# A four-stage per-sample pipeline on one Trainium2 core: the software-pipelined loop cut at another place, the gate's logits issued among the next scores, and two places where products and transposes are laid out differently

## The chip, the cores and the metric

The kernel runs on one core of a Trainium2 chip. The metric is the device time of one execution in microseconds (us); lower is better. The engines are named as the profile names them: PE (TensorE, matrix products), DVE (VectorE), ACT (ScalarE), POOL (GpSimd), and SP (SyncE, which here issues every DMA). Each engine works off its own queue strictly in order, and engines wait for one another on semaphores.

## The reference, cut to what matters

There are 16 samples of 256 tokens by 256 features. Each goes through four residual stages:

```
x = x + x @ W0[subject].T + b0[subject]                       # per-sample linear
x = x + zX*lap_x(x) + zY*lap_y(x) + zR*x*(1-x)                # Laplacian and reaction
q,k,v = projections;  w = softmax([q.k (masked), q.k_own]/4)  # 16 heads of width 16
x = x + (w @ v) @ Wo + bo
h_e = relu(x @ wi_e) @ wo_e, e = chosen, shared0, shared1     # three experts, 1024 wide
g = softmax(relu([h_e at token 0] @ g1) @ g2)                 # gate: three logits a sample
x = x + g0*h_chosen + g1*h_shared0 + g2*h_shared1
```

## The kernel before

Operands in float32 are split into a rounded "hi" part and a "lo" rest, and a product is three matmuls: hi*hi, lo*hi, hi*lo (L520 to L522). Splitting costs an ACT copy (hi) and a DVE or POOL subtraction (lo) for each tile.

Each engine has a list of stage names, written out by hand (`PE_BODY`, `ACT_BODY`, `DVE_BODY`, `POOL_BODY`, `SP_BODY`). One pass through the lists is a turn, and a turn works on up to three samples at once: `lag(name)` says how many samples behind the turn's number a stage is. Turns 0 and 1 are unrolled, turns 2 to 15 are a hardware loop (`Fori`), turns 16 and 17 are unrolled again. In the steady state every engine repeats its list once per sample.

The stages that matter:

- **S0 to S15**: the scores of one head, for the row maxima (PE L623, two matmuls; DVE L987 reduces them). After S7 and S15 DVE makes the maxima into three bf16 parts (L994 to L1000), **m0/m1** transposes them on PE, ACT copies them out, and SP's DMA L451 (`q_rows<-max_rows`) puts them under the queries. The first exponential of each half, E0 and E8, waits for that DMA (`max_placed`).
- **E0 to E15**: the scores again with mask and maxima (PE L636), then ACT's exponential twice (L833 in float32, L837 in float16; for heads 11, 13 and 15 DVE makes the float16 copy, L1006), and the rest `prob_lo` on DVE (heads 1, 3, 5, 7, 11, 13, 15; L1007) or POOL (the others; L1208). Right behind E(h) PE issues `attend(h-2)`, eight small matmuls that need `prob_lo` of head h-2.
- **H0 to H11 and P0 to P11**: the experts' first and second layer in twelve steps (12 products each). H(s) on ACT makes `hid_hi` (L873), on DVE `hid_lo` (L1067). H(s) on PE waits for the split of H(s-2), P(s) for that of H(s). Experts 0 and 1 are shared, steps 8 to 11 are the chosen one, whose weights are loaded for each sample.
- **wi0 to wi3, wo0 to wo3**: the chosen expert's weights. SP loads a quarter into `raw`, ACT makes `exp_hi` (L849), POOL `exp_lo` (L1151). The load of wo n (L403) goes into the place of wi n and waits until POOL has split it.
- **load**: SP's five DMAs for the next sample (weights, x, side input, bias, coefficients).
- **aT, wo, x3_parts**: attention's result is transposed on PE (L548), split with the bias (ACT L864, DVE L1048), multiplied with Wo, and added (DVE L1060); ACT L881 and DVE L1063 split that sum for the experts, and H0 waits for it.
- **gate, relu, logits, mix, scale, sum**: PE L696, DVE L1086, PE L701 (logits), DVE L1090 and L1091, ACT exponential, DVE L1095 to L1097 (mix), then DVE L1055 (scale), ACT L890 twice, POOL L1180 and L1182 (sum), and SP's store.
- **kp, k3** on SP: from the end of E15 SP issues 13 DMAs (mask, six `q_rows`, six `k_rows`) that place the next sample's queries and keys. S0 waits for all of them.

`RING` is the list of the PE stages that use the two banks `front0` and `front1` in turn (S, E, m, x1, q, lap, ks, vs, kp, vp, self). A stage waits until the stage two places before it in that list has been read out (`open_bank`).

The loop begins with H0 in every list. The order around the places that change is, before:

```
PE:  ... aT vp wo gate self logits | H0 S0 S1 H1 S2 S3 P0 S4 S5 H2 S6 S7 P1 H3 S8 S9 P2 m0 H4 S10 S11 P3 H5
     E0 S12 E1 P4 E2 S13 H6 E3 S14 P5 E4 S15 H7 E5 P6 E6 m1 ... E11 E12 kp E13 P9 E14 H11 E15 P10
SP:  ... k3 sum | load wo0 wo1 wo2 wo3 m0 m1 wi_load E15 kp k3 sum
POOL: ... ks vp sum | wi0 wi1 wi2 wi3 wo0 x_parts wo1 ...
```

Of the kernel before, what the change touches and what calls it, by code (L numbers as in the profile page):

```python
# [24 lines left out]
ACT = mybir.ActivationFunctionType  # L25
# [7 lines left out]
P = 128  # L33
# [21 lines left out]


PE_BODY = """
H0 S0 S1 H1 S2 S3 P0 S4 S5 H2 S6 S7 P1 H3 S8 S9 P2 m0 H4 S10 S11 P3 H5
E0 S12 E1 P4 E2 S13 H6 E3 S14 P5 E4 S15 H7 E5 P6 E6 m1 H8 E7
x1 P7 q E8 H9 E9 lap P8 E10 H10 E11 E12 kp E13 P9 E14 H11 E15 P10 ks pvend P11  # L60
vs aT vp wo gate self logits
""".split()
ACT_BODY = """
H0 wi0 x3_keep H1 wi1 H2 wi2 wi3 H3 wo0 m0 H4 wo1 x_parts P3 H5 w_parts E0 E1 wo2 E2 H6 E3 wo3 E4 H7 E5 s_parts E6 m1 H8 E7
x1_parts react q E8 P7 H9 E9 qa E10 x2_parts H10 E11 qb E12 kp E13 kq E14 H11 E15 ks P11
vs aT vp x3_parts x2b logits sum
""".split()
DVE_BODY = """
S0 S1 H0 S2 S3 H1 S4 S5 S6 H2 S7 S8 H3 S9 x_parts S10 H4 S11 S12 H5 E1 S13 gate0 H6 S14 E3 S15 H7 E5 H8 E7
x1 x1_parts react H9 half lap gate1 x2_parts H10 E11 kp E13 k3 H11 E15  # L70
att aT gate2 vp wo x3_parts relu self logits mix scale
""".split()
POOL_BODY = """
wi0 wi1 wi2 wi3 wo0 x_parts wo1 w_parts E0 wo2 E2 wo3 E4 s_parts E6 m1 x1 E8 E9 qa E10 norm qb E12 E14 ks vp sum
""".split()
SP_BODY = """
load wo0 wo1 wo2 wo3 m0 m1 wi_load E15 kp k3 sum
""".split()

S_OF, E_OF = [f"S{h}" for h in range(H)], [f"E{h}" for h in range(H)]  # L80
PRESENT = "load x_parts w_parts s_parts x1 x1_parts react q qa qb lap x2_parts ks vs kp kq k3 vp x2b self".split()
PREVIOUS = S_OF + E_OF + "m0 m1 half norm pvend att aT wo x3_parts wi_load".split()


def lag(name):
# [18 lines left out]

SHARED_AT = ["ks", "vp", "E0", "E2", "E4", "E6", "m1", "E8"]
SHARED = len(SHARED_AT)
SP_FIRST = "load wo0 wo1 wo2 wo3 m0 E0 E2 E4 E6 m1 wi_load E15 kp k3 vp sum".split()
assert [x for x in SP_FIRST if x in SP_BODY] == SP_BODY
LIN_ORDER = [0, 1, 2, 3]
PARTS = 2 * STEPS  # L110
# [17 lines left out]

BQ, BK, BO, BV, B_PREV, B_SELF, NVEC = range(7)

LINKS = {"early": 4, "attention": 4 + 5 + len(HI_DVE), "rest": 8}


def wait(eng, sem, per_turn, turn, n):
# [7 lines left out]
def build(nc, x, side, seq_len, subject, label, z, w0, b0, wqkvo, vecs, wi, wo, swi, swo,  # L142
          g1, g2, consts, iota, out):
    with ExitStack() as ctx:
# [233 lines left out]
        def _(sp):  # L378
# [43 lines left out]
            def stage(name, i):  # L422
# [10 lines left out]
                elif name == "E15":  # L433
                    wait_filled(sp, i, name)
                elif name == "kp":
                    sp.dma_start(k_rows[MASK_ROW:MASK_ROW + 1, :, :],
                                 mask_dram[bass.ds(i, 1), :].unsqueeze(1).to_broadcast([1, H, S])).then_inc(mask_placed, 16)
                    wait(sp, q_split, 1, i, 1)
                    place(q_rows, Q_BANDS, q_parts, 0, q_placed)
                    place(q_rows, Q_BANDS, q_parts, 1, q_placed)  # L440
                    place(q_rows, Q_BANDS, q_parts, 2, q_placed)
                    wait(sp, k_part_done, 2 * C, i, 2 * C)
                    place(k_rows, K_BANDS, k_parts, 0, k_placed)
                    place(k_rows, K_BANDS, k_parts, 1, k_placed)
                elif name == "k3":
                    wait(sp, k_split, 1, i, 1)
                    place(k_rows, K_BANDS, k_parts, 2, k_placed)
                elif name in ("m0", "m1"):
                    half = int(name[1])
                    wait_freed(sp, i, name)  # L450
                    sp.dma_start(q_rows[ROWS_MAX:ROWS_EXP, half * HALF:(half + 1) * HALF, :], max_rows[:, :]).then_inc(max_placed, 16)  # L451
                elif name == "wi_load":
                    kind = chooser(label_sb, i, wi.shape[0])
                    wait(sp, w_split, PARTS, i, SHARED)
                    load_wi(kind)
                elif name[0:2] == "wo":
# [60 lines left out]
        def _(pe):  # L517
# [124 lines left out]
            def hidden(s, j):  # L642
# [110 lines left out]
        def _(act):  # L753
# [158 lines left out]

        @block.vector
        def _(dve):
            link_sems = {"early": early_link, "attention": attention_link, "rest": rest_link}
            linked = dict.fromkeys(LINKS, 0)

            def link(ins, stretch, seq):
# [121 lines left out]
            def rest(name, j):  # L1040
# [238 lines left out]
```

## Time and profile before

| | |
|---|---|
| median of three runs | 1175.02 us (1174.24 to 1176.38) |
| the profiled execution | 1179.7 us, of which the span of its instructions 1177.9 us |
| PE busy (matmuls) | 1028.2 us, 87% of the span |
| PE weight loads | 955.5 us, 81% |
| DVE | 818.1 us, 69% |
| ACT | 682.4 us, 58% |
| POOL | 634.3 us, 54% |

Busy shares are averages over the whole span. Matmuls are pipelined, so PE's busy time is not time at its peak. The clock column of a view is the granted TensorE clock, 1.00 for 2.4 GHz and 0.50 for 1.2 GHz. A releaser behind "<-" is what ended an engine's idle time.

### The profile page before, as it was taken

The numbers are of one execution on the slowest core, as the hardware profiler recorded it, in microseconds if no ns is written. First come the engines' busy times: TensorE is split into PE (matmuls) and PEld (weight loads), VectorE is DVE, ScalarE is ACT, GpSimd is POOL, SyncE is SP. The second block draws the span as 40 slices with busy tenths as digits, with TensorE's granted clock in tenths as the row PEclk, the third lists the DMA queues.
The fourth block names the chain that finished last, engine by engine and source line by source line (L and its number), as shares of the span: only waits on it lengthen the run. The fifth ranks groups of instructions, "written<-read, shape, count | busy, mean of one in ns | idle before, by whom it ended". The sixth has DMA issues, their size and how long they took to land.

```text
span 1177.9 us, 27595 instructions
## 1 busy us (share of the span) xinstructions
PE 1028.2 (87%) x9488; PEld 955.5 (81%) x9488; DVE 818.1 (69%) x1616; ACT 682.4 (58%) x1401; POOL 634.3 (54%) x544
## 2 busy tenths in 40 slices
PE   3658989999898999899899999989989998998986
PEld 3347878888888888888788888878888887888886
DVE  3475776777777777767777776777777777867632
ACT  2463655747466564746566574656657475665632
POOL 5492645637464564736466473646647364654531
PEclk8667998999999999999999999999999999999978
DMA  4636152171524216152522615242251624234110
GB/s 137 114 108 99 45 67 72 37 124 36 63 77 70 78 47 115 36 69 82 64 72 52 109 36 83 78 54 72 58 104 36 91 70 54 72 63 73 38 45 9
DMA packets 91387, 82.67 MB, mean 70 GB/s; under 512 B 11972, under 2 KB 90852, under 8 KB 91364
## 3 DMA queue, kind: packets, MB, share of 16 engines
q1 hardware_dynamic: 91364, 82.37, 34.8%
q8 instruction: 14, 0.23, 0.1%
q14 instruction: 9, 0.07, 0.0%
HBM read 52.58 MB, written 4.20 MB: 48 GB/s over the span
## 4 chain that ended last, share of the span: by engine, by line
POOL 30%; issue 27%; PE 23%; DVE 13%; ACT 5%; DMA 1%; POOLq 1%; SPq 0%; DVEq 0%; ACTq 0%
POOL exp_lo L1151 10%; POOL prob_lo L1208 10%; PE out L520 3%; DVE prob_lo L1007 3%; PE out L522 3%; PE out L521 3%; PE hid L520 2%; PE hid L521 2%; PE hid L522 2%; PE front L520 2%; POOL e_out L1180 2%; PE front L522 2%; PE front L521 1%; POOL s_lo L1161 1%; PE pv L578 1%
## 5 line engine op out<-in xcount | busy, mean ns | idle before, releaser
L520 PE MATMUL hid<-x_hi,exp_hi 128*128 128x256 f32 x768 | 239.9, 312 | 1.4 <-DVE x_lo L1063 1.4
L1208 POOL TENSOR_TENSOR prob_lo<-prob,prob_hi 128x512 f16<-128x512 f32 x144 | 182.8, 1270 | 88.3 <-ACT prob_hi L837 87.1
L520 PE MATMUL out<-hid_hi,exp_hi 128*128 128x256 f32 x768 | 229.2, 298 | 0.0
L522 PE MATMUL hid<-x_hi,exp_lo 128*128 128x256 f32 x768 | 225.7, 294 | 0.0
L521 PE MATMUL hid<-x_lo,exp_hi 128*128 128x256 f32 x768 | 225.7, 294 | 0.0
L1151 POOL TENSOR_TENSOR exp_lo<-raw,exp_hi 128x512 fp32r<-128x512 f32 x128 | 163.8, 1290 | 109.7 <-ACT exp_hi L849 109.7
L987 DVE TENSOR_REDUCE s_max<-front 128x2 f32<-128x512 f32 x256 | 171.6, 687 | 68.9 <-PE front L623 67.1
L521 PE MATMUL out<-hid_lo,exp_hi 128*128 128x256 f32 x768 | 215.4, 280 | 0.0
L522 PE MATMUL out<-hid_hi,exp_lo 128*128 128x256 f32 x768 | 215.2, 280 | 0.0
L873 ACT ACTIVATE hid_hi<-hid 128x512 fp32r<-128x512 f32 x192 | 115.4, 601 | 168.4 <-PE hid L522 167.0
L1067 DVE SCALAR_TENSOR_TENSOR hid_lo<-hid,hid_hi 128x512 fp32r<-128x512 f32 x192 | 131.5, 685 | 104.0 <-ACT hid_hi L873 102.2
L833 ACT ACTIVATE prob<-front 128x512 f32<-128x512 f32 x256 | 153.2, 599 | 33.6 <-PE front L636 32.4
L520 PEld LDWEIGHTS hid<-x_hi,exp_hi 128*128 128x128 f32 x768 | 154.7, 201 | 5.6 <-DVE x_lo L1063 1.5
L521 PEld LDWEIGHTS hid<-x_lo,exp_hi 128*128 128x128 f32 x768 | 155.5, 202 | 0.0
L522 PEld LDWEIGHTS hid<-x_hi,exp_lo 128*128 128x128 f32 x768 | 154.3, 201 | 0.0
L520 PEld LDWEIGHTS out<-hid_hi,exp_hi 128*128 128x128 f32 x768 | 145.4, 189 | 3.8 <-DVE hid_lo L1067 1.9
L521 PEld LDWEIGHTS out<-hid_lo,exp_hi 128*128 128x128 f32 x768 | 145.6, 190 | 0.0
L522 PEld LDWEIGHTS out<-hid_hi,exp_lo 128*128 128x128 f32 x768 | 145.2, 189 | 0.0
L1007 DVE TENSOR_TENSOR prob_lo<-prob,prob_hi 128x512 f16<-128x512 f32 x112 | 112.9, 1008 | 36.7 <-ACT prob_hi L837 35.1
L636 PE MATMUL front<-q_rows,k_rows 100*128 100x256 bf16 x512 | 102.7, 284 | 32.7 <-ACT prob_hi L837 29.2
L837 ACT ACTIVATE prob_hi<-front 128x512 f16<-128x512 f32 x208 | 125.1, 602 | 0.0
L578 PE MATMUL pv<-v_cols,prob_hi 128*128 128x49 bf16 x1024 | 86.8, 186 | 21.2 <-DVE prob_lo L1007 10.6
(162 smaller groups left out, 2311.1 us busy)
## 6 DMA issues: line engine op xcount, KB each, us to landing
raw<-in_wi SPq DMA_DIRECT2D x64, 256.0 KB, 3.7
raw<-in_wo SPq DMA_DIRECT2D x64, 256.0 KB, 2.9
q_rows<-w_raw SPq DMA_DIRECT2D x80, 128.0 KB, 4.3
k_rows<-x1T SPq DMA_DIRECT2D x48, 128.0 KB, 6.6
k_rows<-x_raw SPq DMA_DIRECT2D x48, 128.0 KB, 7.9
x_raw<-in_x SPq DMA_DIRECT2D x16, 256.0 KB, 3.1
w_raw<-in_w SPq DMA_DIRECT2D x16, 256.0 KB, 2.8
s_raw<-in_side SPq DMA_DIRECT2D x16, 256.0 KB, 3.7
```

Of the source, the lines that this page charges most:

```text
L520: nc.tensor.matmul(acc, w_hi, a_hi, start=first, stop=False)
L521: nc.tensor.matmul(acc, w_hi, a_lo, start=False, stop=False)
L522: return nc.tensor.matmul(acc, w_lo, a_hi, start=False, stop=last)
L636: last = nc.tensor.matmul(psum[:, k * S:(k + 1) * S], k_rows[0:ROWS_EXP, h, k * P:(k + 1) * P], q_rows[0:ROWS_EXP, h, :], start=True, stop ...
L833: last = nc.scalar.activation(prob[:, h % NPROB, :], psum[:, :], ACT.Exp, scale=SCALE)
L837: last = nc.scalar.activation(prob_hi[:, h % NPROB, :], psum[:, :], ACT.Exp, scale=SCALE)
L873: nc.scalar.activation(hid_hi[:, s % 2, :], hid_bank[s % 2][:, :], ACT.Relu).then_inc(hid_hi_done, 1)
L987: nc.vector.tensor_reduce(s_max[:, :, h:h + 1], psum, AX_X, ALU.max).then_inc(freed["S"], 1)
L1007: nc.vector.tensor_tensor(prob_lo[:, h % NPROB, :], prob[:, h % NPROB, :], prob_hi[:, h % NPROB, :], ALU.subtract).then_inc(prob_split_dve, 1)
L1067: nc.vector.scalar_tensor_tensor(hid_lo[:, s % 2, :], hid_bank[s % 2][:, :], 0.0, hid_hi[:, s % 2, :].bitcast(F32), ALU.max, ALU.subtract) ...
L1151: nc.gpsimd.tensor_tensor(lo, source, hi.bitcast(F32), ALU.subtract).then_inc(w_split, 1)
L1208: nc.gpsimd.tensor_tensor(prob_lo[:, h % NPROB, :], prob[:, h % NPROB, :], prob_hi[:, h % NPROB, :], ALU.subtract).then_inc(prob_split_poo ...
```

## The change

Three things are done at once.

**The loop is cut elsewhere.** H0 to H3, P0, P1 and S0 to S7 with all that belongs to them move from the start of each list to its end, with their lags lowered by one, so the steady order of most stages is the same and the turn's boundary lies between H3 and S8. Around it some orders do change: on PE the logits go from before H0 to behind S1; on DVE logits, mix and scale are spread among S0 to S4; on POOL sum goes from ahead of wi0 to between wi1 and wi2; on ACT it goes behind H1; and SP issues the four loads of wo ahead of the store, and only then `load` for the next sample and m0's DMA.

**Exponentials are spaced by products.** P4 goes between E0 and E1, and H6, P5, H7 and P6 between the following ones, which leaves E5, E6 and m1 next to each other. Later P9 goes between E11 and E12, and H11 between E13 and E14, which leaves E14 and E15 next to each other. DVE's x_parts goes behind H7, its gate1 behind x2_parts. ACT's w_parts goes behind E1.

**Attention is turned over two banks.** The four transposes write both halves of `pv` in place of one bank, ACT signals after each half, and DVE starts on the first half while ACT copies the second.

```diff
 PE_BODY = """
-H0 S0 S1 H1 S2 S3 P0 S4 S5 H2 S6 S7 P1 H3 S8 S9 P2 m0 H4 S10 S11 P3 H5
-E0 S12 E1 P4 E2 S13 H6 E3 S14 P5 E4 S15 H7 E5 P6 E6 m1 H8 E7
-x1 P7 q E8 H9 E9 lap P8 E10 H10 E11 E12 kp E13 P9 E14 H11 E15 P10 ks pvend P11
-vs aT vp wo gate self logits
+S8 S9 P2 m0 H4 S10 S11 P3 H5 E0 S12 P4 E1 S13 H6 E2 S14 P5 E3 S15 H7 E4 P6 E5 E6 m1 H8 E7
+x1 P7 q E8 H9 E9 lap P8 E10 H10 E11 P9 E12 kp E13 H11 E14 E15 P10 ks pvend P11
+vs aT vp wo gate self H0 S0 S1 logits H1 S2 S3 P0 S4 S5 H2 S6 S7 P1 H3
 """.split()
 ACT_BODY = """
-H0 wi0 x3_keep H1 wi1 H2 wi2 wi3 H3 wo0 m0 H4 wo1 x_parts P3 H5 w_parts E0 E1 wo2 E2 H6 E3 wo3 E4 H7 E5 s_parts E6 m1 H8 E7
-x1_parts react q E8 P7 H9 E9 qa E10 x2_parts H10 E11 qb E12 kp E13 kq E14 H11 E15 ks P11
-vs aT vp x3_parts x2b logits sum
+m0 wo0 H4 wo1 x_parts P3 H5 E0 E1 w_parts H6 E2 wo2 E3 H7 wo3 E4 E5 s_parts E6 m1 H8 E7
+x1_parts react q E8 P7 H9 E9 qa E10 x2_parts H10 E11 qb E12 kp E13 kq H11 E14 E15 ks P11
+vs aT vp x3_parts x2b H0 logits wi0 H1 sum wi1 x3_keep H2 wi2 wi3 H3
 """.split()
 DVE_BODY = """
-S0 S1 H0 S2 S3 H1 S4 S5 S6 H2 S7 S8 H3 S9 x_parts S10 H4 S11 S12 H5 E1 S13 gate0 H6 S14 E3 S15 H7 E5 H8 E7
-x1 x1_parts react H9 half lap gate1 x2_parts H10 E11 kp E13 k3 H11 E15
-att aT gate2 vp wo x3_parts relu self logits mix scale
+S8 S9 S10 H4 S11 S12 H5 E1 S13 gate0 H6 S14 E3 S15 H7 x_parts E5 H8 E7
+x1 x1_parts react H9 half lap x2_parts gate1 H10 E11 kp E13 k3 H11 E15
+att aT gate2 vp wo x3_parts relu self S0 S1 logits H0 S2 mix S3 H1 scale S4 S5 S6 H2 S7 H3
 """.split()
 POOL_BODY = """
-wi0 wi1 wi2 wi3 wo0 x_parts wo1 w_parts E0 wo2 E2 wo3 E4 s_parts E6 m1 x1 E8 E9 qa E10 norm qb E12 E14 ks vp sum
+wo0 x_parts wo1 E0 w_parts E2 wo2 E4 wo3 s_parts E6 m1 x1 E8 E9 qa E10 norm qb E12 E14 ks vp wi0 wi1 sum wi2 wi3
 """.split()
 SP_BODY = """
-load wo0 wo1 wo2 wo3 m0 m1 wi_load E15 kp k3 sum
+load m0 m1 wi_load E15 kp k3 wo_load0 wo_load1 wo_load2 wo_load3 sum
 """.split()
...
+PRESENT += S_OF[:HALF]
-PREVIOUS = S_OF + E_OF + "m0 m1 half norm pvend att aT wo x3_parts wi_load".split()
+PREVIOUS = S_OF[HALF:] + E_OF + """m0 m1 half norm pvend att aT wo x3_parts x3_keep H0 H1 H2 H3 P0 P1
+wi_load wi0 wi1 wi2 wi3 wo_load0 wo_load1 wo_load2 wo_load3""".split()
...
-                transposed(pv_bank[0], att).then_inc(att_turned, 1)
+                transposed(pv, att).then_inc(att_turned, 1)
...
-                    psum = chunked(pv_bank[0])
-                    for c in range(C):
-                        last = nc.scalar.activation(ak_hi[:, c, :], psum[:, c, :], ACT.Identity, bias=vec[:, c, BV:BV + 1])
-                    last.then_inc(att_hi_done, 1)
+                    for c in range(C):
+                        nc.scalar.activation(ak_hi[:, c, :], pv[:, c, 0:S], ACT.Identity, bias=vec[:, c, BV:BV + 1]).then_inc(att_hi_done, 1)
...
-                    wait(dve, att_hi_done, 1, j, 1)
-                    psum = chunked(pv_bank[0])
-                    for c in range(C):
+                    for c in range(C):
+                        wait(dve, att_hi_done, C, j, c + 1)
```

Waits for the shared experts' weights are put at the first step of each, in place of one wait at H0; after the first sample they are long met.

## Rows read from the trace of the kernel before

**Rows 1.** Busy time of each engine in one steady turn (windows)

```profile
437.00:505.20 68.20, 62.28 (x593) 58.41 (x593) 50.47 (x100) 41.98 (x88) 37.97 (x33) 0.97 0.36 70
```

**Rows 2.** Timeline of PE: E15 of two samples, one turn apart

```profile
437.54 0.39 PE L636 MATMUL front<-q_rows,k_rows 100*128 100x256 bf16 x2
...
505.80 0.39 PE L636 MATMUL front<-q_rows,k_rows 100*128 100x256 bf16 x2
```

**Rows 3.** Timeline of PE: logits, H0, S0, m0, E0

```profile
451.50 0.82 PE L701 MATMUL out<-gate,gate_h 128*128 128x3 f32 x4 [1.69 <-DVE gate_h L1086]
452.19 0.56 PE L520 MATMUL hid<-x_hi,exp_hi 128*128 128x256 f32 x1
...
454.90 0.74 PE L623 MATMUL front<-k_rows,q_rows 97*128 97x256 bf16 x4
...
466.10 0.28 PE L629 MATMUL front<-ident_half,m_parts 128*24 128x128 bf16 x2
...
471.13 0.39 PE L636 MATMUL front<-q_rows,k_rows 100*128 100x256 bf16 x2
```

**Rows 4.** Windows: H0, with the granted clock third from the end

```profile
451.70:455.10 3.40, 3.40 (x17) 3.27 (x17) 1.68 (x6) 1.54 (x3) 0.00 (x0) 0.51 0.26 24
```

**Rows 5.** SP's last `k_rows` issues, and landing of the tile's DMAs

```profile
444.72 1.90 SPq L420 DMA_DIRECT2D k_rows<-x_raw  x3
...
DMA to landing us min/median/max: 2.1/7.0/8.1
```

**Rows 6.** Timeline of SP: store, `load`, the wo loads, m0's DMA

```profile
457.93 0.42 SPq L463 DMA_DIRECT2D out<-e_out  x1
...
459.87 0.39 SPq L390 DMA_DIRECT2D w_raw<-in_w  x1
...
463.31 3.97 SPq L403 DMA_DIRECT2D raw<-in_wo  x4
467.42 0.86 SPq L451 DMA_DIRECT2D q_rows<-max_rows  x1
```

**Rows 7.** The chain that ended last: m0's DMA, issue to landing

```profile
50.98 2.31 DMA q_rows<-max_rows
```

**Rows 8.** Timeline of POOL: sum, then wi0 and wi1

```profile
455.12 1.28 POOL L1180 TENSOR_TENSOR e_out<-e_out 128x512 f32<-128x512 f32 x1 [4.68 <-ACT e_out L890]
...
457.72 2.52 POOL L1151 TENSOR_TENSOR exp_lo<-raw,exp_hi 128x512 fp32r<-128x512 f32 x2
```

**Rows 9.** Timeline of DVE around the logits and the first scores

```profile
450.36 0.69 DVE L1063 TENSOR_TENSOR x_lo<-x3T,x_hi 128x512 fp32r<-128x512 f32 x1 [0.70 <-ACT x_hi L881]
...
453.05 0.16 DVE L1095 TENSOR_REDUCE gate_s<-gate_s 128x1 f32<-128x3 f32 x1 [0.27 <-ACT gate_s L878]
...
453.71 0.75 DVE L1055 SCALAR_TENSOR_TENSOR e_out<-e_out,gate_s,x_kept 128x512 f32<-128x512 f32 x1
455.46 1.29 DVE L987 TENSOR_REDUCE s_max<-front 128x2 f32<-128x512 f32 x2 [1.00 <-PE front L623]
```

**Rows 10.** Timeline of PE: E1, kp, E13, attend(11)

```profile
473.47 0.39 PE L636 MATMUL front<-q_rows,k_rows 100*128 100x256 bf16 x2 [1.73 <-ACT prob_hi L837]
...
499.71 0.36 PE L520 MATMUL front<-x_hi,lin_hi 128*128 128x256 f32 x1 [1.14 <-DVE x_lo L929]
...
501.22 0.40 PE L636 MATMUL front<-q_rows,k_rows 100*128 100x256 bf16 x2
...
502.13 0.20 PE L578 MATMUL pv<-v_cols,prob_hi 128*128 128x49 bf16 x1 [0.51 <-DVE prob_lo L1007]
```

**Rows 11.** Timeline of DVE: gate0, E3, gate1, x2_parts

```profile
477.06 1.27 DVE L1082 SCALAR_TENSOR_TENSOR gate_terms<-gate,e_out,gate_terms 128x256 f32<-128x256 f32 x1
...
479.65 1.78 DVE L1007 TENSOR_TENSOR prob_lo<-prob,prob_hi 128x512 f16<-128x512 f32 x1
...
496.02 2.40 DVE L1082 SCALAR_TENSOR_TENSOR gate_terms<-gate,e_out,gate_terms 128x256 f32<-128x256 f32 x2
498.46 1.10 DVE L929 TENSOR_TENSOR x_lo<-react,x_hi 128x512 fp32r<-128x512 f32 x1
```

More of the change, by code:

```diff
@@ L106 @@
 SHARED = len(SHARED_AT)
-SP_FIRST = "load wo0 wo1 wo2 wo3 m0 E0 E2 E4 E6 m1 wi_load E15 kp k3 vp sum".split()
+SP_FIRST = "load m0 E0 E2 E4 E6 m1 wi_load E15 kp k3 vp wo_load0 wo_load1 wo_load2 wo_load3 sum".split()
 assert [x for x in SP_FIRST if x in SP_BODY] == SP_BODY
@@ L129 @@
 BQ, BK, BO, BV, B_PREV, B_SELF, NVEC = range(7)
-LINKS = {"early": 4, "attention": 4 + 5 + len(HI_DVE), "rest": 8}
+LINKS = {"early": 4, "maxima0": 2, "maxima1": 2, "attention": 5 + len(HI_DVE), "rest": 8}
 def wait(eng, sem, per_turn, turn, n):
@@ L328, in build @@
         early_link = sem("early_link")
+        maxima_link = [sem("maxima0_link"), sem("maxima1_link")]
         attention_link = sem("attention_link")
@@ L455, in stage @@
                     load_wi(kind)
-                elif name[0:2] == "wo":
-                    n = int(name[2])
+                elif name[:-1] == "wo_load":
+                    n = int(name[-1])
                     kind = chooser(label_sb, i, wo.shape[0])
@@ L547, in transposed @@
                     for t in range(C):
-                        last = nc.tensor.transpose(psum[:, c * S + t * P:c * S + (t + 1) * P],
-                                                   src[:, t, c * P:(c + 1) * P], ident[:, :])
+                        last = nc.tensor.transpose(psum[:, c, t * P:(t + 1) * P], src[:, t, c * P:(c + 1) * P], ident[:, :])
                 return last
@@ L647, in hidden @@
                     wait(pe, x3_split, 1, j, 1)
-                    pe.wait_ge(w_split, SHARED)
                     pe.wait_ge(gate_in, 32)
+                if s % STEPS == 0 and e < CHOSEN:
+                    pe.wait_ge(w_split, 4 * e + 2)
                 if e == CHOSEN:
@@ L666, in project @@
                 wait(pe, hid_split, LSTEPS, j, s + 1)
+                if s % STEPS == 0 and e < CHOSEN:
+                    pe.wait_ge(w_split, 4 * e + 4)
                 if s == 0:
@@ L914, in _ @@
         def _(dve):
-            link_sems = {"early": early_link, "attention": attention_link, "rest": rest_link}
+            link_sems = {"early": early_link, "maxima0": maxima_link[0], "maxima1": maxima_link[1], "attention": attention_link, "rest": rest_link}
             linked = dict.fromkeys(LINKS, 0)
@@ L925, in linkf @@
                 def linkf(ins):
-                    link(ins, "early" if name in EARLY else "attention", i)
+                    link(ins, "early" if name in EARLY else f"maxima{int(name[1:]) // HALF}" if name[0] == "S" else "attention", i)
                 def rest_of(src, hi, lo):
@@ L1044, in rest @@
                 if name == "aT":
-                    wait(dve, att_hi_done, 1, j, 1)
-                    psum = chunked(pv_bank[0])
                     for c in range(C):
-                        last = nc.vector.scalar_tensor_tensor(ak_lo[:, c, :], psum[:, c, :], vec[:, c, BV:BV + 1],
+                        wait(dve, att_hi_done, C, j, c + 1)
+                        last = nc.vector.scalar_tensor_tensor(ak_lo[:, c, :], pv[:, c, 0:S], vec[:, c, BV:BV + 1],
                                                               ak_hi[:, c, :].bitcast(F32), ALU.add, ALU.subtract)
```

## The prediction

> **What bounds the kernel now.** I read the page first, then one steady turn in windows, then the timelines of PE, DVE, ACT, POOL and SP through that turn, and SP's landings. The reader is to see three things. First, PE is the engine that sets the turn: busy 62.28 of 68.20 us, DVE 50.47, ACT 41.98, POOL 37.97 [rows 1]. The turn is 505.80 - 437.54 = 68.26 us [rows 2], and 13 of the 16 samples go through it in full. Second, PE's few waits are where the change aims. The logits wait 1.69 us for the gate, and H0 behind them starts at 452.19 [rows 3], in a stretch of 3.40 us granted 0.51 of the clock, the lower level of 1.2 GHz [rows 4]. E1 waits 1.73 us for ACT, kp 1.14 for DVE, attend(11) 0.51 for DVE [rows 10]. Third, two things that no wait of PE shows, since they are just hidden: SP's DMAs for queries and keys, and SP's place in line for m0's DMA.
>
> **Part 1, from E15 to S0: gains 0.7 us a turn, not 3.** Before, S0 stands 454.90 - 437.54 = 17.36 us after E15 [rows 2, 3]. With the logits behind S1, H0 waits only for the split of its input, which DVE ends at 450.36 + 0.69 = 451.05 [rows 9]; H0 takes 1.5 us at the full clock (twelve products, as kp's 499.71 to 501.22 [rows 10]). So S0 could come at 452.6, 2.3 us earlier, and turning attention over two banks would bring a few tenths on top. But S0 also waits for the DMAs. The last of the `k_rows` issues starts at 444.72 + 1.90 - 0.60 = 446.0 and lands 8.1 us later [rows 5], at 454.1, that is 16.6 us after E15; that series begins when E15 is filled, in the new order too. So S0 comes at E15 + 16.65: -0.7 us. The earlier H0, the two banks (they lie ahead of this landing, so I cost them at nothing; without that cover they gain up to 0.4) and H0's half clock (1.3 us, hidden too) all end at this one DMA. Bounds: 0 to -0.8.
>
> **Part 2, from S0 to E0: loses 4.0 us.** Before it is 471.13 - 454.90 = 16.2 us [rows 3]. Follow the new order, times after S0. DVE reduces S0 and S1 from 0.56 to 1.85 [rows 9]; the logits' two small steps end near 2.3 and H0's rest near 2.9. PE has issued logits (0.5) and H1 (1.5), so S2 reaches DVE at 2.95 and is reduced at 3.6; mix takes 453.71 - 453.05 = 0.66 [rows 9], so the gate stands at 4.25. Behind that:
>
> - POOL does wi1 only after ACT, whose list has sum's two scalings first. They took 455.12 - 453.71 = 1.4 us from the gate to POOL [rows 8, 9], so 5.65; ACT's wi1 0.6, to 6.25. POOL: wi1 1.26, sum 457.72 - 455.12 = 2.6, wi2 and wi3 2.52 [rows 8]: 6.25 + 1.26 + 2.6 + 2.52 = 12.65.
> - SP may issue the last wo load only then. Behind it in SP's queue stand the store, `load` with five DMAs, and m0's DMA. From the store's issue to the first wo load it now takes 463.31 - 457.93 = 5.4 us, with the look-up of 0.9 that belongs to wo; then the four wo loads, 467.42 - 463.31 = 4.1 [rows 6]. New: one wo load's issue 0.6, and 5.4 - 0.9 + 0.1 = 4.6 to m0's. So m0's DMA goes at 12.65 + 5.2 = 17.85, wherever the maxima are.
> - It lands 2.31 later [rows 7], at 20.15. E0 waits for it: E0 at 20.2, against 16.2: +4.0.
>
> PE alone would be slower here too: logits 0.5, and S5, S6 and S7 wait some 0.35 each for banks, because DVE has mix and scale (0.75 [rows 9]) between the reductions; that makes m0 stand near 12.6 instead of 466.10 - 454.90 = 11.2 [rows 3], and E0 could go at 17.6. That is the lower bound, +1.4; the upper one is +4.6 (SP at 5.8). I take +4.0, since POOL's and SP's work is counted piece by piece from rows. Behind the waiting E0 in PE's queue stand S12, P4 and everything else. The same delay of `load` holds up ACT's x_parts, and P3 and H5 behind it, until near 19.5; that is just hidden by E0's wait.
>
> **Part 3, from E0 to x1: between -1.9 and +1.0, taken +0.4.** E1's wait of 1.73 [rows 10] goes, since P4 fills it: about -1.9 with its start. But taking P4 ahead of E1 leaves less PE work behind E1 for DVE to catch up. From E1 DVE does prob_lo, S13, gate0, H6 and S14, which ended at 479.65 [rows 11], 6.2 us after E1 at 473.47 [rows 10]. S15 needs that bank, and PE now comes to it 4.4 us after E1; DVE is then some 0.5 faster, since S13 waits less, so about 1.35 is given back. Then E4, E5, E6 and m1 come with P6 alone between them: ACT has H7 and wo3's copy (0.6 each) ahead of E4, then POOL 1.2 for its rest, and attend(4) behind E6 waits about 1.0.
>
> DVE's times here swing: prob_lo was 1.78 us at 479.65 while POOL worked, and gate0's step 1.27 [rows 11]. The Trainium skill says in "SBUF — State Buffer", section "Who interferes with whom", that a DVE instruction with two SBUF inputs contends with a GpSimd instruction that reads SBUF; the trace's long ones agree. By that rule moving DVE's and POOL's work onto each other costs up to 1.1 a time, and part 3 would be +1.0.
>
> **Part 4, from x1 to E15: -0.75 us.** Up to E10 nothing moves. Before, kp waits 1.14 for `x_lo`, which stood behind gate1 (2.40 us from 496.02), and attend(11) waits 0.51 [rows 10, 11]. New: P9 goes ahead of E12 and x2_parts ahead of gate1, so kp waits for nothing. But attend(11) needs DVE's E11, and DVE's list up to there is the same work with an idle start, up to 0.9 until ACT's copy is there: attend(11) comes at best as now, at worst 0.9 later. Behind it one product fewer (1.5) stands before E15. So -1.5 to -0.5; I take -0.75. H11, E14 and E15 then follow with nothing waiting.
>
> **Sum.** -0.7 + 4.0 + 0.4 - 0.75 = +2.95 us a turn, to 71.2. Sample 2 to 14 see it in full: 13 x 2.95 = 38. Of the others, S0's sample 1 has no sum yet and sample 15 no `load` (about +1 each), and the last sample's tail, with no scores, gains 1.5 from the earlier H0. Together +39. The profiled execution, 1179.7 us (span 1177.9 and 1.8 around it), would become 1218.7. It lies 4.7 above the median of the three runs, so against 1175.0 I get 1214 us. The waits at S0 (2 us) and E0 (2.5 us) are new idle time of PE, and products behind such a wait can run at the lower clock, as H0 does today [rows 3, 4]; one such stretch costs 1.3 when nothing hides it. I add 2 us for a tenth of them and forecast 1216.
>
> **The rivals, and the forecast among them.**
>
> - **The forecast (0.50):** 1200 to 1230, by the bounds of the parts.
> - **The clock makes it worse (0.13).** Idle before the logits preceded the 3.40 us at 0.51 [rows 3, 4]. Two waits of that length a turn, each followed by dense products, cost 1.3 each: up to 13 x 2.6 = +34, and with one 13 x 1.3 = +17: 1231 to 1248. For it: E0's wait is longer than today's 1.69. Against: E1's wait of 1.73 today is followed by no low clock (the turn as a whole is at 0.97 [rows 1], which the one stretch explains). The Trainium skill, "TensorE: Matmul & The Clock Gate", section "HAM oscillation — how this bites in real kernels", describes a loop whose waits for DMAs throttle the products behind each of them; by it this rival is what would happen.
> - **Spacing pays in full (0.20).** Parts 3 and 4 at their best, -1.9 and -1.5: -0.7 + 4.0 - 1.9 - 1.5 = -0.1 a turn; with one of the two at its best, about +0.8 to +2: 1176 to 1200. For it: E1's wait is plain to see. Against: DVE's catching up.
> - **Faster (0.13).** SP's queue is not what E0 waits for: m0's DMA goes by 15.3 after S0 (17.6 - 2.31), so 2.5 us sooner than I count, for example because sum on POOL ends before wi1 is there. Then part 2 is +1.4 and the turn -0.7 + 1.4 + 0.4 - 0.75 = +0.35, and it turns to a gain from the point where part 3 gives back less than 1.5 of its 1.9; at best -0.7 + 1.4 - 1.9 - 1.5 = -2.7 a turn, 1140. Against: SP's order is fixed, and its issues have a measured length.
> - **No change within 0.2% (0.04)**, which is about what a measurement of this kernel can tell: gains and losses cancel.
>
> **Range and chances.** The cases from 1180 up to 1243 hold 8 in 10: it leaves out the faster rival and the far end of the clock's. Slower by over 0.2%: 0.50 + 0.13 + nearly all of 0.20 = 0.82; same 0.05; faster 0.13.
>
> **What would show it.** S0 waits for the DMA `k_rows<-x_raw`, with H0 ended well before. E0 waits 2 to 3 us for `q_rows<-max_rows`, whose issue follows `load`'s DMAs on SP without a pause. The logits don't wait. E1 doesn't wait, S15 and attend(4) wait for DVE and POOL. kp doesn't wait, attend(11) does. The turn is near 71 us. I am wrong if E0 doesn't wait, or if S0 comes less than 16.5 us after E15.

## The result and the profile after

The changed kernel takes 1277.5 us (median of four, 1258.5 to 1278.9) against 1175.7 for the kernel before. The ratio is 1.077, 95% interval 1.062 to 1.092; it leaves out two of the four runs, 1278.7 and 1278.9, which count as slow beside the 1258.5. Slower was right, the size was not: 1216 was forecast, with 1243 as the upper end. The profiled execution has a span of 1274.4 us against 1177.9, 96.5 more.

Where it went is read from PE's timeline, by the starts of the same instructions in each turn. The table has medians over 12 steady turns; "warm" is e7_warm (below), the changed kernel with PE kept busy in two waits. The forecast's E0 is taken as m0 + 7.6 (20.2 - 12.6).

| stretch, us | before | forecast | after | warm |
|---|---|---|---|---|
| E15 to aT | 6.8 | | 7.3 | 6.8 |
| aT to S0 | 10.5 | | 9.8 | 10.0 |
| (E15 to S0) | 17.3 | 16.65 | 17.1 | 16.8 |
| S0 to m0 | 11.2 | 12.6 | 16.1 | 14.3 |
| m0 to E0 | 5.0 | 7.6 | 6.5 | 6.5 |
| E0 to x1 | 15.0 | 15.4 | 15.2 | 15.2 |
| x1 to E15 | 19.7 | 18.9 | 20.3 | 19.3 |
| turn | 68.2 | 71.2 | 75.1 | 72.2 |

PE's timeline of one turn after; it answers to [rows 3, 10]:

```profile
478.93 0.38 PE L522 MATMUL hid<-x_hi,exp_hi 128*128 128x256 f32 x1 [1.28 <-DVE x_lo L1064]
...
482.36 1.03 PE L624 MATMUL front<-k_rows,q_rows 97*128 97x256 bf16 x4 [1.36 <-DMA k_rows<-x_raw]
483.19 0.85 PE L705 MATMUL out<-gate,gate_h 128*128 128x3 f32 x4
...
498.48 0.28 PE L630 MATMUL front<-ident_half,m_parts 128*24 128x128 bf16 x2 [1.91 <-DVE s_max L989]
...
505.04 0.39 PE L637 MATMUL front<-q_rows,k_rows 100*128 100x256 bf16 x2 [1.36 <-DMA q_rows<-max_rows]
...
517.76 0.20 PE L579 MATMUL pv<-v_cols,prob_hi 128*128 128x49 bf16 x1 [0.83 <-POOL prob_lo L1209]
...
537.36 0.20 PE L579 MATMUL pv<-v_cols,prob_hi 128*128 128x49 bf16 x1 [1.81 <-DVE prob_lo L1009]
```

The waits named in the prediction are there: S0 for the keys' DMA, E0 for the maxima's, S15 for DVE (0.4, and S14 as much), attend(4) for POOL, attend(11) for DVE; logits, E1 and kp don't wait. E0's is 1.36 us and not the 2 to 3 that were named, because another wait stands ahead of it that was not expected at this size: m0, 1.91 us for DVE.

The same turn in windows, the granted clock third from the end; it answers to [rows 1, 4]:

```profile
472.60:547.80 75.20, 65.31 (x593) 60.24 (x592) 51.08 (x100) 41.99 (x87) 37.61 (x33) 0.93 0.32 63
478.90:480.00 1.10, 1.07 (x9) 1.07 (x10) 0.47 (x3) 0.05 (x1) 0.00 (x0) 1.00 1.15 116
480.10:486.80 6.70, 5.34 (x26) 4.75 (x25) 2.18 (x5) 1.32 (x3) 1.28 (x1) 0.50 0.07 6
486.90:538.00 51.10, 43.91 (x427) 40.27 (x426) 37.24 (x67) 32.74 (x66) 32.57 (x28) 1.00 0.21 62
538.10:541.40 3.30, 3.30 (x29) 2.96 (x28) 2.33 (x5) 1.99 (x5) 0.00 (x0) 0.50 0.00 0
```

Before, 3.4 us of a turn ran at 1.2 GHz. Now it is 6.7 us around S0, and 3.3 us more behind the wait of attend(11). The first stretch begins at 480.1, inside H0, 1.2 us behind H0's wait and ahead of S0's; it holds all of S0's wait and reaches through H1 behind it.

SP's timeline, as [rows 6]: from the last wo load to m0's DMA it waits for nothing, 502.41 - 497.04 = 5.4 us. ACT had the maxima ready at 499.25 (second fence), 3.2 us ahead of that DMA.

```profile
497.04 0.38 SPq L405 DMA_DIRECT2D raw<-in_wo  x1
497.62 0.40 SPq L465 DMA_DIRECT2D out<-e_out  x1
499.76 0.39 SPq L392 DMA_DIRECT2D w_raw<-in_w  x1
...
501.93 0.34 SPq L396 DMA_DIRECT2D z_sb<-in_z  x1
502.41 0.87 SPq L453 DMA_DIRECT2D q_rows<-max_rows  x1
```

```profile
498.88 0.37 ACT L828 ACTIVATE max_rows<-front 24x256 bf16<-24x256 bf16 x1 [3.52 <-PE front L630]
```

DVE and POOL while DVE takes the first half's maxima apart (timelines of each):

```profile
493.25 1.03 DVE L996 SCALAR_TENSOR_TENSOR s_max<-s_max,s_self 128x16 f32<-128x16 f32 x1
494.32 1.21 DVE L998 TENSOR_SCALAR m_parts<-s_max 128x16 bf16<-128x16 f32 x1
495.56 1.21 DVE L999 SCALAR_TENSOR_TENSOR m_rest<-s_max,m_parts 128x16 f32<-128x16 f32 x1
496.69 0.16 DVE L1000 SCALAR_TENSOR_TENSOR m_parts<-s_max,m_parts 128x16 bf16<-128x16 f32 x1
```

```profile
491.58 1.30 POOL L1181 TENSOR_TENSOR e_out<-e_out 128x512 f32<-128x512 f32 x1
492.95 1.30 POOL L1183 TENSOR_TENSOR e_out<-e_out 128x512 f32<-128x512 f32 x1
494.21 2.53 POOL L1152 TENSOR_TENSOR exp_lo<-raw,exp_hi 128x512 fp32r<-128x512 f32 x2
```

Steps of 16 elements a partition take 1.0 to 1.2 us while POOL works, and end when POOL's instruction ends (494.28 and 494.25; 496.77 and 496.74). With POOL free the next one takes 0.16.

### The profile page after: what moved, and what is told of

Read it like the earlier page. It is cut to its first block, busy times and chain, and to the rows that moved or that the text cites. A ratio compares the mean times of both kernels' runs of the same rounds, so it can differ in the third digit from the quotient of the medians.

```text
span 1274.4 us, 27693 instructions
## 1 busy us (share of the span) xinstructions
PE 1068.2 (84%) x9488; PEld 982.6 (77%) x9488; DVE 826.0 (65%) x1616; ACT 681.8 (53%) x1401; POOL 627.4 (49%) x544
## 4 chain that ended last, share of the span: by engine, by line
issue 35%; PE 29%; POOL 19%; DVE 8%; ACT 4%; DMA 2%; SPq 1%; POOLq 1%; ACTq 0%; DVEq 0%
POOL exp_lo L1152 9%; PE hid L522 4%; POOL prob_lo L1209 3%; PE hid L524 3%; PE hid L523 3%; PE front L637 2%; PE out L522 2%; DVE prob_lo L1009 2%; PE out L523 2%; PE out L524 2%; PE front L522 2%; PE front L524 2%; PE front L523 2%; DMA k_rows<-x_raw 2%; PE pv L579 2%
## 5 line engine op out<-in xcount | busy, mean ns | idle before, releaser
L522 PE MATMUL hid<-x_hi,exp_hi 128*128 128x256 f32 x768 | 245.4, 319 | 21.1 <-DVE x_lo L1064 21.1
L1209 POOL TENSOR_TENSOR prob_lo<-prob,prob_hi 128x512 f16<-128x512 f32 x144 | 173.5, 1205 | 179.1 <-ACT prob_hi L841 178.4
L524 PE MATMUL hid<-x_hi,exp_lo 128*128 128x256 f32 x768 | 233.7, 304 | 0.0
L523 PE MATMUL hid<-x_lo,exp_hi 128*128 128x256 f32 x768 | 232.0, 302 | 0.0
L522 PEld LDWEIGHTS hid<-x_hi,exp_hi 128*128 128x128 f32 x768 | 159.5, 208 | 26.6 <-DVE x_lo L1064 22.7
L524 PEld LDWEIGHTS hid<-x_hi,exp_lo 128*128 128x128 f32 x768 | 161.2, 210 | 0.0
L523 PEld LDWEIGHTS hid<-x_lo,exp_hi 128*128 128x128 f32 x768 | 160.9, 210 | 0.0
L624 PE MATMUL front<-k_rows,q_rows 97*128 97x256 bf16 x512 | 101.9, 310 | 43.1 <-DMA k_rows<-x_raw 25.2
L579 PE MATMUL pv<-v_cols,prob_hi 128*128 128x49 bf16 x1024 | 90.5, 190 | 51.3 <-DVE prob_lo L1009 31.7
L579 PEld LDWEIGHTS pv<-v_cols,prob_hi 128*128 128x128 f16 x1024 | 75.3, 100 | 69.1 <-DVE prob_lo L1009 36.4
```

What stands on the lines that cost most here:

```text
L522: nc.tensor.matmul(acc, w_hi, a_hi, start=first, stop=False)
L523: nc.tensor.matmul(acc, w_hi, a_lo, start=False, stop=False)
L524: return nc.tensor.matmul(acc, w_lo, a_hi, start=False, stop=last)
L579: nc.tensor.matmul(acc, prob_hi[:, h % NPROB, at:at + P], v_cols[:, k, h, :], start=(k == 0), stop=False)
L624: last = nc.tensor.matmul(psum[:, t * S:(t + 1) * S], q_rows[0:ROWS_MAX, h, t * P:(t + 1) * P], k_rows[0:ROWS_MAX, h, :], start=True, stop ...
L1209: nc.gpsimd.tensor_tensor(prob_lo[:, h % NPROB, :], prob[:, h % NPROB, :], prob_hi[:, h % NPROB, :], ALU.subtract).then_inc(prob_split_poo ...
```

## The experiments

Ratios are to the kernel before, run beside each on the same chip. Stretches are medians over 12 steady turns, as in the table.

### One part of the change at a time

All four have the loop cut between H3 and S8.

**e1_cut**: the cut alone.

```diff
-PE:  ... gate self H0 S0 S1 logits H1 ...        (as changed)
+PE:  ... gate self logits H0 S0 S1 H1 ...        (all orders as before)
-SP:  load m0 ... k3 wo_load0..3 sum
+SP:  load wo_load0..3 m0 ... k3 sum              (wo_load two samples behind)
```

> Only the loop is cut between H3 and S8; all orders of work around it are those of before (save that DVE does H3 ahead of S8), attention turned in one bank. If the loss comes from the orders, the cut is free: 1175 us, within 6. Rival, the new cut costs something itself, because every engine now branches in the middle of dense work: 0.5 us or more for each of 14 turns, 1182 us or more.

Measured 1193.2 us, ratio 1.013 (1.009 to 1.017). The rival's size, but see e5_cut_s8 and e9b_cut_warm.

**e2_spacing**: e1_cut with the changed orders from S8 to P11.

> The cut kernel with the exponentials spaced by products (PE, ACT, DVE and POOL orders between S8 and P11 as in the change), logits and SP as before. Prediction's parts 3 and 4: -0.35 us a turn, 1170 us. Rival, DVE's late E11 brings a wait of attend(11) of 1.8 us and products at 1.2 GHz behind it, as the changed kernel's trace shows: +1.0 us a turn, 1188 us.

Measured 1204.2, 1.024 (1.021 to 1.028), 11 us above e1_cut. Neither number, the rival's mechanism: in turns without slow products behind attend(11), x1 to E15 takes 19.3 us, 0.4 less than before; in the others 20.4.

**e3_logits**: e1_cut with the changed orders from self to H3 on every engine, SP's too.

> The cut kernel with the logits among the next scores, sum between wi1 and wi2 on POOL and the wo loads ahead of the store and load on SP, as in the change; exponentials and attention as before. If nearly all of the loss is here (late m0 DMA and two stretches at 1.2 GHz around S0): +5.9 us a turn, 1250 us. Rival, the loss is shared with the spacing: by the prediction's parts 1 and 2, +3.3 a turn, 1218 us.

Measured 1293.5, 1.100 (1.096 to 1.104), above both numbers: all of the loss is here, and more than all. S0 to m0 takes 15.7 us, m0 to E0 8.0. At least a part of the excess over the changed kernel is not the logits' doing. DVE here still has x_parts between S9 and S10, as before, and waits there for the late `load`; E0 then waits for DVE and not for the maxima (one turn):

```profile
508.23 0.15 DVE L938 TENSOR_SCALAR z_neg<-z_sb 128x1 f32<-128x1 f32 x1 [4.95 <-DMA z_sb<-in_z]
...
510.76 0.39 PE L637 MATMUL front<-q_rows,k_rows 100*128 100x256 bf16 x2 [1.20 <-DVE s_max L991]
```

The changed kernel has x_parts behind H7, and DVE doesn't wait for `load` ahead of E0.

**e4_banks**: e1_cut with attention turned over two banks.

> The cut kernel with attention turned over two banks and nothing else. With the logits ahead of H0 the split of attention lies on PE's path: 0.4 us a turn, 1169 us. Rival, hidden: 1175 us.

Measured 1199.2, 1.018 (1.015 to 1.021), no better than e1_cut, so neither number, since the cut had cost something already. H0 does come 0.36 us sooner after aT (7.23 in place of 7.59), but S0 stands at 10.0, where the keys land.

**e5_cut_s8**: e1_cut, and DVE does S8 ahead of H3 again.

```diff
-DVE: ... S6 H2 S7 H3 | S8 S9 ...
+DVE: ... S6 H2 S7 | S8 H3 S9 ...
```

> The cut alone as in e1_cut, but DVE does S8 ahead of H3 again, as before the change. In e1_cut the stretch from S0 to m0 grew from 11.2 to 12.1 us and nothing else in the median turn. If that is DVE's H3 ahead of S8 (m0 needs the bank that S8 frees): 11.2 again and 1176 us. Rival, the branch of the loop between H3 and S8 costs it: 12.1 stays and so does 1190 us.

Measured 1202.2, 1.023 (1.020 to 1.025): the expectation failed, and so did the rival. In its short turns S0 to m0 is 11.5, so the order on DVE was a part; but more turns are long (seven of twelve, four in e1_cut). A short turn and the long one behind it, in windows, and the long one's stretch right behind E1's wait:

```profile
307.10:375.70 68.60, 62.39 (x594) 58.35 (x593) 50.23 (x100) 42.14 (x87) 38.16 (x33) 0.98 0.36 69
375.70:447.30 71.60, 65.40 (x593) 61.28 (x592) 49.72 (x100) 42.02 (x87) 38.21 (x33) 0.93 0.34 66
...
406.80:410.10 3.30, 3.30 (x18) 3.08 (x18) 0.69 (x1) 1.60 (x3) 2.40 (x3) 0.50 0.00 0
```

The same instructions, DVE, ACT and POOL equally busy within 0.6 us, and 3.0 us apart, which is PE's extra busy time. The long turns have slow products behind S0 (S0 to m0 12.7) and behind E0 (E0 to x1 16.5 in place of 15.0). E1's wait is 1.7 us in all twelve turns, and the clock falls behind it in seven. This asks for a test of the clock by itself.

### The clock by itself

The added products write the idle second hidden bank (at E1 the first) from constant weights.

```diff
+def keep_busy(n):
+    for _ in range(n):
+        nc.tensor.matmul(hid_bank[1][:, 0:S], lin_hi[:, 0, 0:P], lin_hi[:, 0, 0:S], start=True, stop=True)
...
+keep_busy(8)     # at S0, ahead of the wait for its DMAs
+keep_busy(12)    # at attend(11), ahead of its wait
```

**e7_warm**: the changed kernel with these two.

> The changed kernel with added products that nothing reads, in two of PE's waits: 8 ahead of S0's wait for its DMAs and 12 ahead of attend(11). If the low clock behind those two waits costs time of its own: S0 to m0 1.3 us and E14 to aT 1.4 us shorter, 13 x 2.7 = 35 us less: 1241 us. Rival, the slow products only fill time that DVE, POOL and SP would make PE wait anyway: 1270 us or more.

Measured 1238.2, 1.053 (1.051 to 1.056), the expectation. 20 useless products a turn make the kernel 39 us faster than its median and its profiled execution (span 1235.6 for 1274.4), and 20 faster than its one run at 1258.5. That run is itself a sign of the clock: its mean granted clock was 0.924, that of the other three 0.900 to 0.909. The turn is 72.2, its clock 0.98 in place of 0.93:

```profile
461.00:533.40 72.40, 65.20 (x614) 60.92 (x612) 51.20 (x100) 41.77 (x87) 37.62 (x33) 0.98 0.34 66
```

SP's last wo load, m0's DMA and E0 in that turn, whose S0 starts at 471.36:

```profile
484.25 0.38 SPq L405 DMA_DIRECT2D raw<-in_wo  x1
...
489.57 0.87 SPq L453 DMA_DIRECT2D q_rows<-max_rows  x1
...
492.11 0.39 PE L645 MATMUL front<-q_rows,k_rows 100*128 100x256 bf16 x2 [1.24 <-DMA q_rows<-max_rows]
```

**e8_before_warm**: the kernel before, with `keep_busy(10)` ahead of the logits' wait.

> The kernel before, with 10 added products that nothing reads ahead of the logits' wait, so that H0 behind them runs at 2.4 GHz. If the landing of the keys bounds S0, H0's 1.3 us are worth only 0.5 a turn: S0 9.95 us after aT in place of 10.5, 1169 us. Rival, without that bound: 1.3 a turn, 1158 us; rival, the low clock only moves to H1: 1175 us or more.

Measured 1177.2, 1.000 (0.998 to 1.002): nothing, less than the 0.5 a turn expected. The second rival has the number and not the mechanism: the low clock mostly did not move at all. In eight of twelve turns H0 still runs at 1.2 GHz and S0 comes at 10.2 to 10.3; in four H0 runs at the full clock and S0 comes at 10.0, where the keys land, and two of these four pay 1.5 us behind E1's wait instead. H0 of one turn of each kind, in windows:

```profile
316.10:318.50 2.40, 2.40 (x13) 2.40 (x12) 1.68 (x6) 1.23 (x3) 0.00 (x0) 0.53 0.21 19
...
452.40:454.10 1.70, 1.70 (x13) 1.50 (x13) 1.15 (x6) 0.43 (x2) 0.00 (x0) 1.00 0.36 33
```

So this run doesn't test the kernel before at the full clock. Its two turns with no slow stretch at all take 67.6 us, 0.6 less than before. The kernel before has its one slow stretch on H0 in every turn, and the keys hide all but that 0.6.

**e9b_cut_warm**: e5_cut_s8 with 10 products at the logits and 12 at E1.

> The cut alone in the form of e5_cut_s8 (1202 us, whose turns are either 68.5 us or, with slow products behind S0 and behind E0, 71.5), with added products that nothing reads: 10 ahead of the logits' wait and 12 ahead of E1's wait. If the cut costs only because it moves the waits and the low clock behind them onto products that nothing hides: every turn near 68.1, 1173 us. Rival, the branch in its new place costs: 1190 us or more.

Measured 1174.9, 0.999 (0.997 to 1.001). Every turn is 67.7 to 68.6. So the cut itself costs next to nothing (its turns without a slow stretch take 67.9, those of e8_before_warm 67.6); nearly all of what e5_cut_s8 lost was the clock.

**e12b_space**: the kernel before, uncut, with the spacing alone (order as in the change between S8 and P11).

> The kernel before, uncut, with the spacing of the exponentials alone, no added products. By the prediction's parts 3 and 4 it gains a little, 0.35 a turn: 1171 us. Rival, the wait of attend(11) brings the low clock onto the products behind it in some turns, as in e2_spacing: 1180 us or more.

Measured 1194.7, 1.016 (1.014 to 1.019), the rival. Three turns in a row, 68.0, 69.4 and 70.8 us:

```profile
378.90:446.90 68.00, 62.24 (x594) 58.59 (x593) 49.74 (x100) 42.01 (x87) 37.63 (x33) 0.97 0.35 69
446.90:516.30 69.40, 63.63 (x593) 59.84 (x592) 49.80 (x100) 41.94 (x87) 37.63 (x33) 0.95 0.35 68
516.30:587.10 70.80, 65.05 (x594) 61.13 (x593) 49.78 (x100) 42.04 (x87) 37.65 (x33) 0.93 0.36 68
```

**e10b_space_warm**: e12b_space with 10 products at the logits and 12 at attend(11).

> The kernel before, uncut, with the spacing of the exponentials as in the change and added products at two waits (10 ahead of the logits, 12 ahead of attend(11)). Spacing took x1 to E15 from 19.7 to 19.3 and E0 to x1 from 15.0 to 15.1 where the clock was full; with S0 at the landing of the keys the turn is 67.5: 13 x 0.75 = 10 us less than before, 1166 us. Rival, some other wait lowers the clock: 1176 us or more.

Measured 1168.8, 0.994 (0.992 to 0.996): 0.6% faster than the kernel before. Once the clock holds, the spacing takes 0.4 us a turn off x1 to E15 (19.3) and gives 0.1 back from E0 to x1 (15.1); the rest of the gain is S0 at the landing of the keys. This is one of six turns of twelve without a slow stretch; the other six take 68.0:

```profile
441.00:508.30 67.30, 63.67 (x616) 59.88 (x614) 49.73 (x100) 41.68 (x87) 37.65 (x33) 1.00 0.36 71
```

### SP's queue, and what makes m0 late

**e6_m0_act**: the changed kernel, the maxima's DMAs issued by ACT.

```diff
 nc.scalar.activation(max_rows[:, :], ..., ACT.Copy).then_inc(freed["m"], 1)
+wait_freed(act, i, name)
+act.dma_start(q_rows[ROWS_MAX:ROWS_EXP, ...], max_rows[:, :]).then_inc(max_placed, 16)
```

> The changed kernel, with the DMAs of the maxima (m0, m1) issued by ACT right behind its copy, so that they don't stand behind the store and load on SP. If SP's queue is what E0 waits for: m0 to E0 falls from 6.5 to the 5.05 that PE needs, 13 x 1.45 = 19 us less than the changed kernel's 1277: 1258 us. Rival, E0 would be late anyway, because ACT's x_parts waits for load with H5 and E0 behind it: the time reappears between E0 and x1, 1277 us.

Measured 1271.3, 1.082 (1.079 to 1.084), between the two. m0 to E0 fell to 5.05 in most turns, but E0 to x1 rose from 15.2 to 15.9: the rival, for half of it. The 6 us against the changed kernel are less than its own four runs lie apart.

**e11b_after_fixed**: e7_warm with that and with S8 ahead of H3 on DVE.

> e7_warm (1238 us) with two more things undone: the maxima's DMAs are issued by ACT, and DVE does S8 ahead of H3. Prediction's SP queue is then gone: m0 to E0 5.05 in place of 6.5, and S0 to m0 shorter by up to 0.9, unless DVE's small steps beside a busy POOL are what m0 waits for. 13 x 2.3 = 30 us less: 1208 us. Rival, the late load holds up ACT instead: E0 to x1 longer, 1225 us or more.

Measured 1232.1, 1.047 (1.045 to 1.050), again the rival. m0 to E0 is 5.05, a gain of 1.45; E0 to x1 takes 16.0 in place of 15.2, x1 to E15 19.9 in place of 19.3. S8's order brought 0.3. The 0.8 behind E0 is P4's wait for an ACT copy that stands behind x_parts, and x_parts waits for `load`:

```profile
486.25 0.63 ACT L768 ACTIVATE x_hi<-x_raw 128x512 fp32r<-128x512 f32 x1 [2.23 <-DMA x_raw<-in_x]
486.78 0.64 ACT L869 ACTIVATE e_out<-out 128x256 f32<-128x256 f32 x2
...
487.47 0.39 PE L521 MATMUL out<-hid_hi,exp_hi 128*128 128x256 f32 x1 [1.13 <-ACT e_out L869]
```

**f1_nosum**: e7_warm with one column in place of 256 in both of POOL's additions, which leaves the shared experts out of nearly all of the output.

> e7_warm (1238 us, S0 to m0 14.3, m0 to E0 6.5) with POOL's two additions of sum cut down to one column of each half, so that the shared experts are left out of nearly all of the output. POOL is then free 2.6 us sooner and idle when DVE takes the maxima apart. If DVE's small steps wait out POOL's instructions (1.0, 1.2 and 1.2 us in the changed kernel's trace, each ending with one of POOL's): S0 to m0 near 12.4; and if wi3 on POOL sets SP's queue and E0: m0 to E0 5.05. 13 x 3.3 = 43 us less, 1195 us. Rival, it is DVE's own order (mix and scale among the reductions): S0 to m0 stays above 13.5, 1215 us or more.

Measured 1200.6, 1.020 (1.017 to 1.023). S0 to m0 is 12.6, and m0 to E0 still 5.9. Two of DVE's three long steps are short now:

```profile
470.19 0.18 DVE L1004 SCALAR_TENSOR_TENSOR s_max<-s_max,s_self 128x16 f32<-128x16 f32 x1
470.40 1.19 DVE L1006 TENSOR_SCALAR m_parts<-s_max 128x16 bf16<-128x16 f32 x1
471.62 0.17 DVE L1007 SCALAR_TENSOR_TENSOR m_rest<-s_max,m_parts 128x16 f32<-128x16 f32 x1
```

The third was as long in the kernel before:

```profile
463.57 1.20 DVE L996 TENSOR_SCALAR m_parts<-s_max 128x16 bf16<-128x16 f32 x1
```

So POOL's sum costs e7_warm 1.7 us a turn ahead of m0, and without it m0 stands at the 12.6 of the prediction. E0's wait for the DMA is still there, 0.37 us:

```profile
479.31 0.39 PE L645 MATMUL front<-q_rows,k_rows 100*128 100x256 bf16 x2 [0.37 <-DMA q_rows<-max_rows]
```

**f2_logits_only**: the logits behind S1 on PE, the other engines' orders around them as before. The cut, the spacing and the added products are those of e7_warm; attention is turned in one bank, and DVE does S8 ahead of H3.

```diff
-DVE: S0 S1 logits H0 S2 mix S3 H1 scale S4   POOL: vp wi0 wi1 sum wi2 wi3   SP: k3 wo_load0..3 sum | load m0
+DVE: S0 S1 logits mix scale H0 S2 S3 H1 S4   POOL: vp sum wi0 wi1 wi2 wi3   SP: k3 sum | load wo_load0..3 m0
```

> The cut kernel with the spacing and the added products, the logits behind S1 on PE as in the change, but the other engines keep the order of before around them: DVE does mix and scale in one piece behind the logits, POOL sum ahead of wi0, SP store and load ahead of the wo loads. If the place of the logits alone makes m0's DMA late: the store goes at S0 + 7.4, m0's DMA 9.5 later, E0 at S0 + 19.3; turn 70.5, 1206 us. Rival, the place of the logits costs nothing and only the other engines' new orders do: turn 67.7, 1170 us.

Measured 1220.0, 1.037 (1.034 to 1.040); turn 71.2. S0 to m0 13.7, m0 to E0 5.6. E0 comes at S0 + 19.3 as expected, the total is 14 us above. e10b_space_warm, with the logits ahead of H0 and uncut, has 11.1 and 5.0 and takes 1168.8: the place of the logits, with nothing moved around it but what must follow, is worth some 50 us and makes both late. One part is a wait of P0 for DVE, which now has mix and scale ahead of H0's rest:

```profile
472.02 0.38 PE L522 MATMUL out<-hid_hi,exp_hi 128*128 128x256 f32 x1 [1.41 <-DVE hid_lo L1079]
```

**f3_logits_m0act**: the same, m0's DMA from ACT.

> f2_logits_only with the maxima's DMAs issued by ACT, so no longer behind the wo loads. If SP's queue was what made E0 late there: m0 to E0 5.05, S0 to m0 12.2, turn 68.5, 1180 us, which is no better than before, because S0 stays at the landing of the keys. Rival: m0 to E0 stays above 5.5.

Measured 1221.2, 1.038 (1.035 to 1.041). m0 to E0 is 5.05 as expected, S0 to m0 stays at 13.7 (expected 12.2), and x1 to E15 gives back 0.6. Issuing m0's DMA elsewhere is worth nothing here.

## Why the direction was right and the size wrong

**Part 1 held.** S0 comes 16.8 to 17.1 us after E15, at the landing of the keys (16.65 forecast), though H0 starts 1.4 us sooner after aT. The two banks are worth nothing where S0 waits for the keys (e4_banks). In short, the gain aimed at was never there: the wait of 1.69 us at the logits [rows 3] became 1.28 at H0 and 1.36 at S0.

**Part 2 had the right waits, and was short by 2.4 us.** E0 comes 22.6 us after S0, not 20.2, beyond the upper bound (+4.6). Warm it is 20.8, so 1.8 of the 2.4 is the clock: SP's last wo load goes 14.7 us after S0 (497.04 - 482.36), and 12.9 warm (484.25 - 471.36), for the 12.65 counted. Of the other 0.6, SP took 5.4 us for the 5.2 counted, and the DMA landed 2.6 after its issue (502.41 to 505.0) for 2.3. How it divides at m0 was wrong: I had 12.6 for m0 and the rest for SP's queue; DVE's steps beside POOL's sum made m0 itself 1.7 later (f1_nosum), so the DMA added only 1.4 on top (e11b_after_fixed). The step that mis-sized m0 took DVE's maxima at their length of before.

**The late `load` is real.** I called it just hidden. With E0's other wait gone it costs 0.8 (e11b_after_fixed against e7_warm).

**Part 3 held**: +0.2 against +0.4; E1's wait is gone, and the waits of S14 and S15 for DVE (0.4 each) and of attend(4) for POOL (0.8) take most of it back; 1.35 and 1.0 were counted.

**Part 4 came near only at the full clock**: -0.4 warm, against -0.75 and bounds of -1.5 to -0.5. In the changed kernel x1 to E15 is +0.6, and E15 to aT +0.5 on top, with attend(11) waiting 1.81 us (0.51 before) and slow products behind it.

**The step that failed is the last line of the sum**: "I add 2 us for a tenth of them", with 0.13 for the clock. It charged 2 us for the clock, and e7_warm shows 39 (20 against the fastest run of the changed kernel). The rival priced it at up to 34 and was right in kind: two stretches a turn, 2.9 us together (75.1 - 72.2 in the table) for its 2.6. It had the place of one wrong: the second lies behind attend(11) and not behind E0. The argument against it, that E1's wait of 1.73 us is followed by no low clock, does not carry. The very same wait of 1.7 us is followed by it in none of twelve turns of the kernel before, in two of e8_before_warm and in seven of e5_cut_s8. So the length of a wait doesn't tell whether products behind it will be slow; what decides it from turn to turn is not shown by these runs.

The Trainium skill's "TensorE: Matmul & The Clock Gate", section "HAM oscillation — how this bites in real kernels", describes a loop whose waits for DMAs throttle the products behind them in each round. The trace agrees in part: the clock is at 0.50 through S0's wait for the keys' DMA and through H1 behind it, though it fell before that wait began, and it does not fall behind E0's 1.36 us for the maxima's DMA. The waits at H0, m0 and attend(11) are for DVE, and are not of the kind that the section describes. With the clock taken as that rival had it (one to two stretches), the forecast would have been 1231 to 1248.

**The ends of the run were the second error.** The 15 gaps between the attention transposes grew by 90.8 us, 6.9 in each of 12, and 4.9 in the last, where I had about 1, because its S0 to E0 is nearly as late without `load` (21.0 us, 16.3 before). The head grew by 4.0 us and the tail by 1.7, where I had a gain of 1.5; why is not shown.

**What the forecast missed, in sum.** For the profiled execution it was 1220.7, and 1276.3 was measured, 55.6 more. 38.8 of them go when PE is kept busy (e7_warm). Of the 16.8 left, some 14 are an estimate from the steady turns: a warm turn is 4.0 us longer than before, not 2.95, in 13 turns.

Open: what would be left at m0 to E0 if `load` were also moved off SP was not tried; nor was a shorter series of keys' DMAs, the bound of S0; nor the kernel before with its slow stretch gone from every turn.

## What to carry to other kernels

A wait that a hand-ordered kernel shows is often the visible one of several that end close together: before moving work to fill it, find what ends just ahead of it (here the last landing of a DMA, 0.8 us before S0) and follow every queue that the moved stage feeds, to the first instruction that others wait behind. A change of order can move slow-clock stretches onto products that nothing hides, even where the waits keep their length; test orders with PE kept busy in the waits, to see the order's own worth apart from the clock's, and look in the trace whether the slow stretches are really gone.

## What the runs showed of the hardware

- 20 added products a turn that nothing reads took the changed kernel from 1277 to 1238 us; the time at 1.2 GHz fell from 10.8 to 3.4 us a turn, what the kernel before has. In the kernel before, 10 of them changed nothing (ratio 1.000) and left H0 slow in eight of twelve turns, and in the cut kernel 22 took 1202 to 1175.
- The same wait of 1.7 us at E1 is followed by 1.2 GHz in none, two or seven of twelve turns, by kernel (before, e8_before_warm, e5_cut_s8).
- One program has turns of 68.6 and 71.6 us side by side, differing in PE's busy time alone (e5_cut_s8).
- A DVE step on 16 elements a partition took 1.0 to 1.2 us beside a POOL instruction, ending with it, and 0.17 without one. Two of the three long steps read two tiles, as the Trainium skill has it in "SBUF — State Buffer", section "Who interferes with whom". L998, a `tensor_scalar`, reads one; the same section says that this kind contends with GpSimd too where it enters a 2-port mode. No run here shows whether it does.
- With the maxima's DMAs issued from ACT's queue in place of SP's, x1 to E15 took 0.6 us longer (e11b_after_fixed, f3_logits_m0act); the cause was not looked for.
